# An attention and feed-forward layer on eight cores: the first pass over a weight chunk moved ahead of the previous chunk's scales

## What is computed

```python
def _bitlinear(x, w_latent):
    scale = clip(mean(abs(w_latent), axis=1, keepdims=True), 1e-05, None)
    tern = clip(round(w_latent / scale), -1.0, 1.0)
    w = w_latent + (tern - w_latent)
    return x @ (w * scale).T
# attention: queries of all rows, keys and values of 4 sink rows and the last 512
mask = cols <= rows + (t_ctx - t)
x = x + _layernorm(attn(_layernorm(x), Wq, Wk, Wv, Wo))
# feed-forward, 1024 -> 4096 -> 1024
h = _bitlinear(x, w_fc) + gate * (x @ v.T @ fast_b.T @ u.T)
r = maximum(h, 0.0)
x = x + _layernorm(_bitlinear(r * r, w_proj))
```

## Time and profile before

| | us |
|---|---|
| median of the runs | 2723.09 (2721.62 to 2724.55, 2 runs) |
| the profiled execution | 2739.74 |
| its span, on its slowest core (core 7) | 2737.7 |
| spans of the other cores | 2705.6 to 2733.6 |
| busy: TensorE matmuls, VectorE, ScalarE | 1652.9 (60%), 1313.8 (48%), 483.5 (18%) |
| chain that ended last: TensorE, VectorE, issue, DMA, ScalarE | 45%, 27%, 11%, 9%, 7% |

### The profile page before, as it was taken

One profiled execution on the slowest core, in us unless ns is written; L12 is line 12 of the kernel. 1 busy time (PEld: TensorE's weight loads), 2 busy tenths in 40 slices (PEclk: granted clock), 3 DMA queues, 4 the chain that ended last, 5 costly groups with the idle time before them and its releaser, 6 DMA issues.

```text
span 2737.7 us, 32025 instructions; the slowest of 8 cores (2705.6 to 2737.7 us)
## 1 busy us (share of the span) xinstructions
PE 1652.9 (60%) x10888; PEld 1089.2 (40%) x10888; DVE 1313.8 (48%) x2281; ACT 483.5 (18%) x1089; POOL 20.8 (1%) x36
## 2 busy tenths in 40 slices
PE   2343433333333333335497787888888888888886
PEld 1111111111111111111275665667666666666665
DVE  1145555555554455447344444445454454544544
ACT  1112111112112211220111111111111111111111
POOL 0000000000000000000000000000000000000000
PEclk9555555555555555555598898899998999989988
DMA  2101020220101110110101101110000000000000
GB/s 43 31 23 46 31 54 31 54 54 23 31 23 31 39 31 24 30 31 16 46 1 32 32 1 32 32 32 21 11 32 31 32 28 5 32 32 32 31 1 31
DMA packets 49200, 80.52 MB, mean 29 GB/s; under 512 B 12019, under 2 KB 37748, under 8 KB 48004
## 3 DMA queue, kind: packets, MB, share of 16 engines
q1 hardware_dynamic: 28244, 44.60, 5.6%
q0 software_dynamic: 4160, 17.11, 2.6%
q10 hardware_dynamic: 16640, 16.78, 2.0%
HBM read 70.42 MB, written 16.78 MB: 32 GB/s over the span
## 4 chain that ended last, share of the span: by engine, by line
PE 45%; DVE 27%; issue 11%; DMA 9%; ACT 7%; DVEq 1%; ACTq 0%; SPq 0%; POOLq 0%
PE pb L114 44%; DVE stg L114 5%; DMA xtl<-xT 5%; DVE srowp L114 4%; DVE srow L114 4%; DVE lnscr L114 4%; ACT sgn L114 2%; DMA stg<-wpj_st 2%; DVE sgn L114 2%; DMA ctxXg<-ctxT 1%; ACT srow L114 1%; ACT lnscr L114 1%; DVE r2s L114 1%; DVE fsq L114 1%; DVE nmb L114 1%
## 5 line engine op out<-in xcount | busy, mean ns | idle before, releaser
L114 PE MATMUL pb<-xn,Sfc 128*128 128x256 bf16 x4096 | 570.0, 287 | 117.6 <-DVE r2s L114 111.5
L114 PE MATMUL pb<-r2s,Spj 128*128 128x256 bf16 x4096 | 563.9, 288 | 0.0
L114 PEld LDWEIGHTS pb<-xn,Sfc 128*128 128x128 bf16 x4096 | 412.4, 103 | 211.1 <-issue 144.1
L114 DVE TENSOR_TENSOR r2s<-pb,rpp 128x256 bf16<-128x256 f32 x512 | 216.0, 424 | 502.0 <-ACT rpp L114 438.9
L114 PEld LDWEIGHTS pb<-r2s,Spj 128*128 128x128 bf16 x4096 | 417.4, 103 | 93.1 <-issue 26.3
L114 DVE SCALAR_TENSOR_TENSOR lnscr<-stg,sgn 128x1024 bf16<-128x1024 f32 x128 | 156.9, 1226 | 391.4 <-ACT sgn L114 237.8
L114 PE MATMUL pb<-sgn,cvecb 128*1 128x512 bf16 x256 | 128.8, 606 | 292.1 <-DVE lnscr L114 292.1
L114 ACT ACTIVATE rpp<-pb,hsc 128x256 f32<-128x256 f32 x256 | 122.7, 479 | 919.8 <-PE pb L114 894.2
L114 PE MATMUL pb<-lnscr,cvecb 128*1 128x512 bf16 x472 | 206.1, 565 | 72.9 <-ACT lnscr L114 72.0
L114 PE MATMUL pb<-srowp,crows 1*128 1x128 f32 (+1 forms) x128 | 43.6, 436 | 276.3 <-ACT srowp L114 158.4
L114 PEld LDWEIGHTS pb<-srowp,crows 1*128 1x128 f32 x128 | 31.7, 306 | 333.9 <-issue 333.9
(11 more groups left out here) (104 smaller groups left out, 1304.3 us busy)
## 6 DMA issues: line engine op xcount, KB each, us to landing
stg<-wfc_st SPq DMA_DIRECT2D x32, 512.0 KB, 3.6
stg<-wpj_st SPq DMA_DIRECT2D x32, 512.0 KB, 3.7
outT<-stg ACTq DMA_DIRECT2D x16, 1024.0 KB, 8.8
xtl<-xT SPq DMA_DIRECT2D x16, 512.0 KB, 5.5
xtl<-xT POOLq DMA_DIRECT2D x16, 512.0 KB, 9.0
ctxXg<-ctxT SPq DMA_DIRECT2D x8, 256.0 KB, 3.0
wbuf<-wk POOLq DMA_DIRECT2D x2, 1024.0 KB, 11.7
wbuf<-wq POOLq DMA_DIRECT2D x2, 1024.0 KB, 8.1
```

The source lines that it names most:

```text
L114: inst = getattr(engobj, fname)(*args, **kwargs)
```

## The change

A1 is cut in two. A1a holds the load, the first Relu and the first `scalar_tensor_tensor`; A1b holds the first round's matmuls and all of round 2. `prep_step` now starts unit n+1 between A2a and A2b of unit n. The instructions, their operands and their number are the same. Three guards move with them: `plo` is waited for once per round as before, and round 1 of unit n+1 waits for `sgn1a` as set by quantizing n-1.

```diff
-                rounds = [(1.0, ALU.max, ALU.subtract, ones_b, sga, "sgn1a"),
-                          (-1.0, ALU.min, ALU.add, negones_b, sgb, "sgn1b")]
-                for r, (scl, op0, op1, lo_lhsT, sg, sgk) in enumerate(rounds):
...
+                E.gwait("scalar", "sgn1a")
+                E.wait("scalar", f"dS{slot}", cL)
+                E.op("scalar", "activation", sga, stflat, AF.Relu,
+                     scale=1.0, inc="sA")
+                cHiA = E.cnt["sA"]
+                E.gwait("vector", "plo")
+                E.wait("vector", "sA", cHiA)
+                E.op("vector", "scalar_tensor_tensor", plo[:, 0:1024],
+                     stflat, 0.0, sga, ALU.max, ALU.subtract, inc="sV")
+                cLoA = E.cnt["sV"]
+                yield "A1a"
+                E.wait("tensor", "sA", cHiA)
+                E.wait("tensor", "sV", cLoA)
+                E.gwait("tensor", "ST")
+                E.gwait("tensor", "pb4")
...
-                yield "A1"
+                yield "A1b"
...
             def prep_step():
                 nonlocal pi
-                if pi >= len(prep_units):
-                    return
-                kind, idx = prep_units[pi]
-                g = mk_prep(kind, idx)
+                if cur_g[0] is None:
+                    if pi >= len(prep_units):
+                        return
+                    cur_g[0] = mk_prep(*prep_units[pi])
+                    pi += 1
+                    next(cur_g[0])
+                g = cur_g[0]
                 next(g)
                 if prev_g[0] is not None:
                     adv(prev_g[0])
                 next(g)
+                if pi < len(prep_units):
+                    cur_g[0] = mk_prep(*prep_units[pi])
+                    pi += 1
+                    next(cur_g[0])
+                else:
+                    cur_g[0] = None
                 next(g)
                 prev_g[0] = g
-                pi += 1
```

More of the change, by code:

```diff
@@ new lines, in gen @@
+                yield "A1a"
[3 more added lines that the diff above has]
+                E.gwait("tensor", "pb4")
+                E.op("tensor", "matmul", ST[0:1, 0:512], ones_b,
+                     sga[:, 0:512], start=True, stop=False)
+                E.op("tensor", "matmul", pbk[4][0:1, 0:512], ones_b,
+                     sga[:, 512:1024], start=True, stop=False)
+                E.op("tensor", "matmul", ST[0:1, 0:512], ones_b,
+                     plo[:, 0:512], start=False, stop=False)
@@ new lines, in gen @@
+                E.op("tensor", "matmul", pbk[4][0:1, 0:512], ones_b,
+                     plo[:, 512:1024], start=False, stop=False, inc="sP")
+                E.gset("plo", "sP")
+                E.gset("sgn1a", "sP")
+                E.gwait("scalar", "sgn1b")
+                E.op("scalar", "activation", sgb, stflat, AF.Relu,
+                     scale=-1.0, inc="sA")
+                cHiB = E.cnt["sA"]
+                E.gwait("vector", "plo")
+                E.wait("vector", "sA", cHiB)
@@ new lines, in gen @@
+                E.op("vector", "scalar_tensor_tensor", plo[:, 0:1024],
+                     stflat, 0.0, sgb, ALU.min, ALU.add, inc="sV")
+                cLoB = E.cnt["sV"]
+                E.wait("tensor", "sA", cHiB)
+                E.wait("tensor", "sV", cLoB)
+                E.op("tensor", "matmul", ST[0:1, 0:512], ones_b,
+                     sgb[:, 0:512], start=False, stop=False)
+                E.op("tensor", "matmul", pbk[4][0:1, 0:512], ones_b,
+                     sgb[:, 512:1024], start=False, stop=False)
@@ L714, in gen @@
+                E.op("tensor", "matmul", ST[0:1, 0:512], negones_b,
+                     plo[:, 0:512], start=False, stop=True)
+                E.op("tensor", "matmul", pbk[4][0:1, 0:512], negones_b,
+                     plo[:, 512:1024], start=False, stop=True, inc="sP")
+                E.gset("plo", "sP")
+                E.gset("sgn1b", "sP")
                 cSt = E.cnt["sP"]
-                yield "A1"
+                yield "A1b"
                 E.gwait("vector", "srowp")
@@ L825, in build_nc @@
             prev_g = [None]
+            cur_g = [None]
             def prep_step():
                 nonlocal pi
-                if pi >= len(prep_units):
-                    return
-                kind, idx = prep_units[pi]
-                g = mk_prep(kind, idx)
+                if cur_g[0] is None:
[5 more added lines that the diff above has]
+                g = cur_g[0]
                 next(g)
```

## The result

The changed kernel takes 2666.5 us (median of 11 runs) against 2727.3 us (10 runs of the kernel before, beside it). The ratio is 0.976, with a 95% interval from 0.974 to 0.979: faster by 65 us, give or take 7. It is the ratio of the means of the fast runs, 2666.7 to 2731.5 us, and not of the two medians, because it leaves out two runs of the changed kernel in which the cores of one die showed a lower clock. The forecast was 65 us and 2658 us; its ratio, 2658 to 2723.1, is 0.976 too.

The account below looks back on a forecast made before the run. The preparation was taken as a chain of waits, with 292.1 us of TensorE idle before the `sgn` matmuls. Terms of 11.7, 10.3, 12.0, 0 and 31.1 sum to 65 us, from 2723.1 to 2658 us; range 2640 to 2680.

Parts of the forecast that it names:

- Terms 1 and 2: First rounds behind K and Q units: idle of 3.39 and 3.01 goes, broadcast 1.72 later; gains 11.7 and 10.3 us.
- Term 3: First round of odd fc units: starts 0.75 us earlier, `plo` and the bank late next; 12.0 us gained.
- Term 4: First round of odd pj units: stays bound by load, Relu and VectorE; gain 0.
- Term 5: First rounds behind heads follow directly, the moved VectorE instruction lying in idle with 0.2 us spare; 31.1 us gained.
- the sign that would have spoken against the forecast: In the heads: a longer chain between their first and last matmul would show the forecast wrong.
- The clock rival: K and Q units: TensorE's clock rises, each gaining 0.50 us, 8 us in all, so 2650; chance 0.10.
- The rival of the held-up head: Heads: the moved VectorE instruction adds 1.23 us to each of 16, 20 us lost, so 2678; chance 0.13.
- the one without effect: The moved Relu is held by `sgn1a` until quantizing n-1 ends, so the wait stays: 2723; chance 0.04.
- The slower one: ScalarE blocked by late loads at 63 places; gain gone at about 4.6 us landing, 2778 at 5.5; chance 0.03.

Follow-up runs that it names:

- heads-only version: The kernel before with the new order used only from the second pj unit on (units 33 to 63): ratio 0.986 to before, stage 1075.6 us.
- three buffers: The change plus a third weight-chunk buffer (`AO`), so a load starts one unit earlier: ratio 0.935 to before, stage 941.4 us; without the change, 0.999.

## Why the prediction was right

The stage can be cut at the first Q matmul and at the first head's first matmul, and the terms re-sorted by where their delay falls: the broadcast before Q unit 0 counts to the K part, that before head 0 to the Q part.

| part | by the terms | measured |
|---|---|---|
| K: 7 x 3.39 - 8 x 1.72 + 8 x 0.75 | 16.0 | 17.1 |
| Q: 8 x 3.01 - 8 x 1.72 + 8 x 0.75 | 16.3 | 16.2 |
| heads: 8 x 3.01 + 8 x 1.09 | 32.8 | 33.9 |
| sum | 65.1 | 67.2 |

- Terms 1 and 2, behind K and Q units: idle gone completely (27.1 to 3.4 us a core, the rest being unit 0, and 24.3 to 0). The delay of the broadcast was priced at 1.72; the idle before it rose from 4.99 to 6.74 in the median, 1.75.
- Term 3, odd fc units: idle 50.6 to 11.9 us a core. The remaining 0.75 of each is ended by the `rbb` copy, which was one of the two things named as late next.
- Term 4, odd pj units: 57.0 and 58.2 us. Nothing gained, as said, and the experiment with three buffers shows why: the load.
- Term 5, heads: complete, 8.9 and 24.3 us a core to 0. The margin of 0.2 us was as thin as said and did not always hold: before a head's first VectorE instruction on core 0, 0.08 to 0.45 us of idle is left in eleven of the fifteen heads from head 1 on, and none in four. It cost nothing that shows: from their first to their last matmul the eight even-numbered heads took 113.0 us in all before and after, the odd-numbered ones 113.3 before and 112.7 after, so the sign that would have spoken against the forecast did not come.
- The bounds were wider than they had to be. The values taken by instructions in the same places were right within 7% in every part.
- The clock rival was in it, smaller than its 8 us. The granted clock is at its upper level more often in the K and Q stage, 0.53 from 307 to 610 us on core 0 where the kernel before had 0.52 from 303 to 387 and 0.50 from 387 to 620 us on core 7, and the group of `sgn` matmuls is busy 3.5 us less. But behind some K units (4 on core 0) the next VectorE instruction then waits for the second round's Relu, which stands behind the unit's copies, and not for the matmuls, so part of it comes back as idle before the second round (49.5 to 51.7 us a core in this stage). Of the 2.1 us by which the sum fell short, 1.1 lie in the heads, where the clock did not change and where the heads-only version gains 33.8 too; so that half is not the clock. How much of the other 1.1, in the K part, is the clock was not tried.
- The rival of the held-up head fell, and so did the one without effect. The slower one is true as a mechanism and missed its condition: landings stayed at a median of 3.6 us. One argument against it did not hold, that the landings of the earlier trace rows had been short "also beside the 1 MB `wbuf` loads"; the last section has what the rows show.

## What to carry to other kernels

When work is moved ahead in an in-order queue, list what is behind it there and what it waits for: a short instruction on the chain (here the Square) should stay in front of one that waits for a load. Read the price of a hidden wait from where it stands: idle of 3.6, 1.09 and 3.39 us in front of the same matmuls was worth 0, 1.09 and 1.7 us in this change. And once engine waits are out, try the buffer again that brought nothing before; here it went from 7 to 101 us.

## What the runs showed beyond that

The landing of a chunk in the changed kernel is not always 3.4 to 3.9 us; its longest in the stage is 5.8 on core 0. On core 0 four fc broadcasts came after 8.8 to 9.2 us of idle instead of 6.7, each while a 1 MB load of `wbuf` was in flight, and the Relu before them started at T+5.05 to T+5.42, some 1.5 us later than the others. Here that load was issued at 463.31, the chunk's at 469.57, and Relu started at 474.65, T+5.16 instead of T+3.6:

```profile
463.31 0.53 POOL L114 DMA_DIRECT2D wbuf<-wq  x1 [108.21 <-PE pb L114]
...
468.26 1.23 DVE L114 SCALAR_TENSOR_TENSOR Sfc<-stg,sgn 128x1024 bf16<-128x1024 f32 x1
...
469.57 0.33 SPq L114 DMA_DIRECT2D stg<-wfc_st  x1
...
474.65 1.06 ACT L114 ACTIVATE sgn<-stg 128x1024 bf16<-128x1024 f32 x1 [10.57 <-DMA stg<-wfc_st]
...
476.05 0.76 PE L114 MATMUL pb<-srowp,crows 1*128 1x128 f32 x2 [8.92 <-ACT srowp L114]
```

In the kernel before, on core 7, no chunk's load was in flight together with a `wbuf` load, and on the other cores three were, over the last 1.2 us of it or less, and landed after 3.4 to 3.7 us. So the rows before could not say how a landing fares beside a `wbuf` load. In the changed kernel five loads meet one on every core, and those 40 landings took 3.5 to 5.8 us. Shortening a period moved two transfers onto each other. I had written that no transfer was added, and had not asked whether two would meet.

It is not the whole story of the landings, though. In the kernel before, cores 2 and 3 had a few of up to 5.2 and 5.1 us with no `wbuf` load of their own in flight, so something else lengthens them too, which was not looked into. Nor does the meeting explain why the changed kernel's cores differ by 8 us in this stage: core 7, at 1045.9 us the slowest there, had landings of 3.5 to 4.3 us at its five meetings, and core 0, with 4.9 to 5.8, took 1044.5. With three buffers no broadcast came late in this way on any core, although two loads a core still met `wbuf` and took up to 4.7 us, since Relu no longer waits for them, and all eight cores lie within 0.7 us of each other.
